# Joint weighted values for the narrow layers, a column bias from one product, a new table of context work, and transposed probabilities copied by ScalarE

## What is computed

```python
# narrow (layers 0 and 3)
q = (rmsnorm(x, norm_w) @ wq).reshape(B, T, 4, 4, 8)
scores = einsum('btgrd,bsgd->bgrts', q, k) / sqrt(8)
out = einsum('bgrts,bsgd->btgrd', softmax(scores), v).reshape(B, T, 128)
x = x + out @ wo
# wide (layers 1 and 2)
col_bias[:, token_indices_A] = -20 * (1 - mask_A)   # one value a row
col_bias[:, token_indices_B] = -20 * (1 - mask_B)   # B wins over A
probs = softmax(q @ k^T / 8 + col_bias)
x = x + (probs @ v) @ Wo + bo
```

## Time and profile before

| | us |
|---|---|
| median of 3 runs | 409.97 (409.69 to 411.9) |
| profiled execution | 409.9 |
| its span, first to last instruction | 408.1 |
| TensorE busy in the span | 380.6 (93%) |
| VectorE, ScalarE, GpSimd busy | 278.2 (68%), 265.8 (65%), 206.7 (51%) |

### The profile page before, as it was taken

The page is one execution under the profiler, slowest core; times in us unless marked ns, Lnnn a source line. Parts: engine busy times, 40 slices in busy tenths (PEclk is TensorE's granted clock), DMA queues, the critical chain, the costliest instruction groups (busy, mean ns, idle before and its releaser), DMA issues.

```text
span 408.1 us, 10552 instructions
## 1 busy us (share of the span) xinstructions
PE 380.6 (93%) x3552; PEld 331.2 (81%) x3552; DVE 278.2 (68%) x1430; ACT 265.8 (65%) x1143; POOL 206.7 (51%) x238
## 2 busy tenths in 40 slices
PE   7999596999999999989999999999999999987775
PEld 6877495899899988968868878888999898866564
DVE  3769955456555756578668877668757756688983
ACT  4585657586657657557477777688777656655870
POOL 5766643254323334468476676345333334567841
PEclk9599898999999999999999999999999999999989
DMA  8700150000000000000000000000000000000000
GB/s 257 323 2 2 45 214 1 2 2 2 2 0 2 2 2 2 2 2 0 2 9 7 8 9 3 0 2 2 2 2 2 2 2 2 0 2 3 6 8 13
DMA packets 4739, 9.71 MB, mean 24 GB/s; under 512 B 592, under 2 KB 3152, under 8 KB 4432
## 3 DMA queue, kind: packets, MB, share of 16 engines
q1 hardware_dynamic: 4400, 8.72, 5.9%
q10 hardware_dynamic: 288, 0.33, 0.3%
HBM read 8.53 MB, written 0.52 MB: 22 GB/s over the span
## 4 chain that ended last, share of the span: by engine, by line
PE 81%; DVE 11%; issue 3%; ACT 3%; DMA 1%; SPq 0%; DVEq 0%
PE pt_ps L791 13%; PE scores_ps L778 9%; PE v_ps L840 8%; PE fill_ps L656 8%; PE fill_ps L658 8%; PE fill_ps L657 8%; PE q_ps L745 7%; PE v_ps L810 7%; PE v_ps L822 7%; PE scores_ps L765 6%; DVE probs L577 6%; ACT probs L462 2%; DVE probsT L588 2%; DVE oT L595 1%; DMA smalls<-in_small 1%
## 5 line engine op out<-in xcount | busy, mean ns | idle before, releaser
L462 ACT ACTIVATE probs<-probs,negmax 128x128 f32<-128x128 f32 x512 | 198.4, 389 | 114.3 <-DVE negmax L577 114.3
L356 POOL TENSOR_TENSOR probs<-probs,inv 128x512 f32<-128x512 f32 x128 | 134.8, 1054 | 186.0 <-DVE inv L584 185.1
L462 ACT ACTIVATION_READ_ACCUMULATOR probs<-probs,negmax 128x1 f32 x512 | 95.6, 187 | 0.0
L577 DVE CUSTOM_DVE_ANT_0 probs<-scores_ps,col_bias,inv_rms 128x128 f32<-128x128 f32 x256 | 73.5, 346 | 21.3 <-PE scores_ps L765 21.1
L577 DVE CUSTOM_DVE_ANT_0 probs<-scores_ps,col_bias 128x128 f32<-128x128 f32 x256 | 58.2, 284 | 41.9 <-PE scores_ps L778 41.9
L588 DVE COPY probsT<-pt_ps 128x512 f32<-128x512 f32 x128 | 82.3, 684 | 5.4 <-PE pt_ps L791 3.4
L791 PE MATMUL pt_ps<-smalls,probs 128*128 128x128 f32 x512 | 72.2, 286 | 0.0
L791 PEld LDWEIGHTS pt_ps<-smalls,probs 128*128 128x128 f32 x512 | 57.0, 145 | 12.6 <-issue 11.3
L810 PE MATMUL v_ps<-probsT,v_narrow 128*32 128x128 f32 x512 | 36.2, 286 | 11.9 <-issue 8.2
L810 PEld LDWEIGHTS v_ps<-probsT,v_narrow 128*32 128x32 f32 x512 | 27.2, 113 | 21.8 <-issue 16.4
L577 DVE DVE_READ_ACCUMULATOR2_ANT negmax<- 128x1 f32 x512 | 43.4, 85 | 0.0
(11 more groups left out here) (90 smaller groups left out, 582.5 us busy)
## 6 DMA issues: line engine op xcount, KB each, us to landing
kT<-in_kv_w SPq DMA_DIRECT2D x6, 512.0 KB, 6.9
w_qo<-in_qo_w SPq DMA_DIRECT2D x2, 1024.0 KB, 9.8
v<-in_ctxT SPq DMA_DIRECT2D x4, 256.0 KB, 3.8
v<-in_kv_w SPq DMA_DIRECT2D x2, 512.0 KB, 11.1
outT<-x SPq DMA_DIRECT2D x8, 64.0 KB, 1.6
x<-in_xT SPq DMA_DIRECT2D x1, 384.0 KB, 8.2
oT<-in_narrow_kv ACTq DMA_DIRECT2D x1, 320.0 KB, 3.0
wn<-in_narrow_w SPq DMA_DIRECT2D x2, 128.0 KB, 4.9
```

Source lines behind the costliest of these rows:

```text
L356: nc.gpsimd.tensor_tensor(p4, p4, inv[:, o % 2, side, :].unsqueeze(2).broadcast_to([P, 4, S]), ALU.mult,).then_inc(probs_made[side], 1)
L462: last = nc.scalar.activation(e, e, ACT.Exp, scale=-1.0, bias=negmax[:, o % 2, side, q:q + 1], accum_out=rowsum[:, o % 2, side, q:q + 1])
L577: last = nc.vector.tensor_tensor_reduce(out=probs[:, o % PROBS_RING, side, cols], in0=scores_ps[side][:, cols], in1=bias, scale=scale, sca ...
```

## The change

It does six things.

- Narrow weighted values are issued once per job, for both octets: 16 products in turn over four column groups, in the half of octet o = 2n + 4. probsT gets a second buffer, by the parity of the octet, for this.
- ScalarE copies the second side of the transposes of all narrow octets, between its first and second four exponentials; VectorE keeps the first side, and both sides of wide octets.
- The column bias: each partition compares its own index (a new column of the small constants) with the tokens, four diagonals are made from it, and one product with mean_w (all 1/128) on TensorE, an entry "bias" in FILLS, spreads them over all rows. VectorE scales the result by 128 x 20 x (1 - mask). bias_made comes after octet 5, SyncE's wait for it is gone, and so are the iota and the comparison of all keys.
- FILLS has other octets for most entries, and the splits of pieces 6 and 7 come an octet later on VectorE, that of piece 0 after octet 0's scores.
- Context 1 is rounded by ScalarE ahead of the loop.
- kn_raw is gone: raw narrow keys go to kn_lo, which is split in place; ScalarE waits for kd_made of the keys two before in place of kn_split. The narrow bias is a broadcast zero (no_bias).

```diff
@@ -78,16 +78,16 @@
...
-    0: ["vn0", "k0.0"], 1: ["kn1.0", "k0.1", "k0.2"], 2: ["k0.3", "v0.0"], 3: ["v0.1", "v0.2", "vn1"],
...
-    24: ["k4.0"], 25: ["k4.1", "kn2.0"], 26: ["k4.2", "vn3"], 27: ["k4.3", "v4.0"], 28: ["v4.1"], 29: ["v4.2", "kn3.0", "v4.3"],
-    30: ["k5.0"], 31: ["k5.1", "k5.2"], 32: ["k5.3"], 33: ["v5.0", "v5.1"], 34: ["v5.2"], 35: ["v5.3", "k6.0"],
...
+    0: ["vn0"], 1: ["k0.0", "kn1.0"], 2: ["k0.1", "k0.2"], 3: ["k0.3", "v0.0"], 4: ["vn1", "v0.1"],
+    5: ["v0.2", "bias"], 6: ["v0.3", "k1.0"], 7: ["k1.1", "k1.2"],
+    8: ["k1.3"], 9: ["v1.0"], 10: ["v1.1", "kn0.3"], 11: ["v1.2", "vn2"], 12: ["v1.3", "k2.0"], 13: ["k2.1"],
...
+    24: ["v3.3"], 25: ["k4.0", "kn2.0"], 26: ["k4.1", "vn3"], 27: ["k4.2"], 28: ["k4.3"], 29: ["v4.0", "kn3.0"],
+    30: ["v4.1", "v4.2"], 31: ["v4.3"], 32: ["k5.0", "k5.1"], 33: ["k5.2"], 34: ["k5.3", "v5.0"], 35: ["v5.1"],
...
+    41: ["v6.1"], 43: ["kn2.3", "v6.2"], 44: ["v6.3"], 45: ["k7.0"], 46: ["k7.1"], 47: ["k7.2"], 48: ["k7.3"],
+    50: ["v7.0"], 53: ["v7.1", "kn3.3"], 55: ["v7.2"], 57: ["v7.3"],
...
@@ -190,7 +191,7 @@
         probs = sb("probs", [P, PROBS_RING, 2, BANK])
-        probsT = sb("probsT", [P, 2, BANK])
+        probsT = sb("probsT", [P, 2, 2, BANK])
         negmax = sb("negmax", [P, 2, 2, 4])
@@ -243,6 +242,10 @@
             return 0 <= o < 2 * NJOBS
+
+        def scalar_copy(o):
+
+            return valid(o) and is_narrow(o // 2)
@@ -268,7 +271,6 @@
             piece(5)
-            sp.wait_ge(bias_made, 1)
             context(2)
@@ -286,8 +288,9 @@
-                pool.wait_ge(c_loaded[p], 16)
-                nc.gpsimd.tensor_copy(c_hi[:, p], c_in[p]).then_inc(rest_rounded, 1)
+                if p > 1:
+                    pool.wait_ge(c_loaded[p], 16)
+                    nc.gpsimd.tensor_copy(c_hi[:, p], c_in[p]).then_inc(rest_rounded, 1)
                 pool.wait_ge(rest_rounded, p)
@@ -313,9 +318,9 @@
                 pool.wait_ge(fill_read[fill_bank(name)], fill_count(name))
-                nc.gpsimd.tensor_copy(kn_hi[:, i % 2], kn_raw[:]).then_inc(kn_rounded, 1)
+                nc.gpsimd.tensor_copy(kn_hi[:, i % 2], kn_lo[:, i % 2]).then_inc(kn_rounded, 1)
                 pool.wait_ge(kn_rounded, i + 1)
-                nc.gpsimd.tensor_tensor(kn_lo[:, i % 2], kn_raw[:], kn_hi[:, i % 2].bitcast(F32), ALU.subtract
+                nc.gpsimd.tensor_tensor(kn_lo[:, i % 2], kn_lo[:, i % 2], kn_hi[:, i % 2].bitcast(F32), ALU.subtract
                                         ).then_inc(kn_split, 1)
@@ -425,9 +429,11 @@
                         return
-                    if i > 1:
-                        act.wait_ge(kn_split, i)
-                    nc.scalar.activation(kn_raw[:], source[:, 0:PAIR], ACT.Copy).then_inc(fill_read[bank], 1)
+                    if i >= 2:
+                        before = KN_ORDER[i - 2]
+                        last = max(n for n, (l, b) in enumerate(JOBS) if f"kn{b // 2}.{l}" == before)
+                        act.wait_ge(kd_made, 2 * narrow_index(last) + 2)
+                    nc.scalar.activation(kn_lo[:, i % 2], source[:, 0:PAIR], ACT.Copy).then_inc(fill_read[bank], 1)
                     return
@@ -470,9 +476,14 @@
                 for name in FILLS.get(o - 1, [])[1:]:
-                    fill_out(name)
+                    if name != "bias":
+                        fill_out(name)
                 if valid(o):
                     exponentials(o, 0)
+                if scalar_copy(o - 2):
+                    act.wait_ge(pt_full[1], o - 1)
+                    nc.scalar.activation(probsT[:, o % 2, 1, :], pt_ps[1][:], ACT.Copy).then_inc(pt_read[1], 1)
+                if valid(o):
                     exponentials(o, 1)
@@ -491,6 +502,8 @@
             round_piece(1)
+            act.wait_ge(c_loaded[1], 16)
+            nc.scalar.activation(c_hi[:, 1], c_in[1], ACT.Copy).then_inc(rest_rounded, 1)
             for n, h in HALVES:
@@ -512,27 +525,29 @@
-                dve.wait_ge(keys_made, 1)
                 dve.wait_ge(tokens_loaded, 16)
-                setup(nc.vector.tensor_copy(key_f, key_i[:]))
                 setup(nc.vector.tensor_copy(tok_f[:, :, 0:2], tok_i[:]))
...
                 setup(nc.vector.tensor_scalar(tok_f[:, :, 2:4], tok_f[:, :, 0:2], float(S), None, ALU.add))
-                shape = [P, LAYER_MASKS, S, 4]
-                setup(nc.vector.tensor_tensor(equal, key_f.unsqueeze(1).unsqueeze(3).broadcast_to(shape),
-                                              tok_f[:].unsqueeze(2).broadcast_to(shape), ALU.is_equal))
+                setup(nc.vector.tensor_scalar(tok_f[:], tok_f[:], key_index, None, ALU.is_equal))
+                setup(nc.vector.tensor_reduce(hits[:].rearrange("p l m -> p (l m)"), tok_f[:], mybir.AxisListType.X, ALU.max))
+                setup(nc.vector.tensor_scalar(only_a[:], hits[:, :, 1], -1.0, 1.0, ALU.mult, ALU.add))
+                setup(nc.vector.tensor_tensor(only_a[:], only_a[:], hits[:, :, 0], ALU.mult))
+                for j in range(4):
+                    on = hits[:, j, 1:2] if j < 2 else only_a[:, j - 2:j - 1]
+                    nc.vector.tensor_scalar(diagonals[:, j, :], identity, on, None, ALU.mult).then_inc(diagonals_made, 1)
...
-                setup(nc.vector.tensor_reduce(hits, equal, mybir.AxisListType.X, ALU.max))
-                of_mask = hits.rearrange("p (l m) s -> p m l s", m=2)
-                setup(nc.vector.tensor_scalar(suppress[:], mask, -SUPPRESS, SUPPRESS, ALU.mult, ALU.add))
-                setup(nc.vector.tensor_scalar(free, of_mask[:, 1], -1.0, 1.0, ALU.mult, ALU.add))
-                setup(nc.vector.tensor_tensor(free, free, of_mask[:, 0], ALU.mult))
-                setup(nc.vector.tensor_scalar(col_bias[:, 0:2, :], of_mask[:, 1], suppress[:, 1:2], None, ALU.mult))
+                bank = fill_bank("bias")
+                setup(nc.vector.tensor_scalar(suppress[:], mask, -SUPPRESS * C, SUPPRESS * C, ALU.mult, ALU.add))
+                dve.wait_ge(fill_full[bank], fill_count("bias"))
+                columns = fill_ps[bank][:].rearrange("p (j s) -> p j s", j=4)
+                setup(nc.vector.tensor_scalar(col_bias[:], columns[:, 0:2], suppress[:, 1:2], None, ALU.mult))
                 setup(nc.vector.scalar_tensor_tensor(
-                    out=col_bias[:, 0:2, :], in0=free, scalar=suppress[:, 0:1], in1=col_bias[:, 0:2, :],
+                    out=col_bias[:], in0=columns[:, 2:4], scalar=suppress[:, 0:1], in1=col_bias[:],
                     op0=ALU.mult, op1=ALU.add))
+                dve.sem_inc(fill_read[bank], 1)
                 dve.sem_inc(bias_made, 1)
@@ -567,7 +582,7 @@
                 l, b = job(n)
-                bias = col_bias[:, 2 if l in NARROW else l - 1, :]
+                bias = no_bias[:].broadcast_to([P, S]) if l in NARROW else col_bias[:, l - 1, :]
                 scale = inv_rms[:, n % 2:n % 2 + 1] if l in NARROW else 1.0
@@ -585,7 +600,7 @@
                 dve.wait_ge(pt_full[side], o + 1)
-                nc.vector.tensor_copy(probsT[:, side, :], pt_ps[side][:]).then_inc(pt_read[side], 1)
+                nc.vector.tensor_copy(probsT[:, o % 2, side, :], pt_ps[side][:]).then_inc(pt_read[side], 1)
@@ -622,19 +637,22 @@
                     transposes_out(o - 2, 0)
-                    transposes_out(o - 2, 1)
+                    if not scalar_copy(o - 2):
+                        transposes_out(o - 2, 1)
+                if o == 0:
+                    split_piece(0)
                 if valid(o):
...
                     match_tokens()
-                if o == 4:
+                if o == 5:
                     column_bias()
-                if o in (5, 6):
-                    split_piece(o + 1)
-
-            nc.vector.memset(col_bias[:, 2, :], 0.0)
+                if o in (6, 7):
+                    split_piece(o)
+
+            nc.vector.memset(no_bias[:], 0.0)
             dve.wait_ge(smalls_loaded, 16)
@@ -688,6 +705,9 @@
                                                 start=(c == 0), stop=(c == CC - 1))
+                elif name == "bias":
+                    pe.wait_ge(diagonals_made, 4)
+                    last = nc.tensor.matmul(out[:], mean_w[:], diagonals.rearrange("p j s -> p (j s)"), start=True, stop=True)
                 elif name.startswith("kn"):
@@ -794,9 +814,11 @@
                 l, b = job(n)
-                if n > 0 and (h == 0 or l not in NARROW):
+                if l in NARROW and h == 0:
+                    return
+                if n > 0:
                     pe.wait_ge(v_read, uses(n, h) - 1)
-                if h == 0 and n > 0:
+                if n > 0 and (h == 0 or l in NARROW):
                     pe.wait_ge(y_read, n)
@@ -804,14 +826,13 @@
                     for r in range(REP):
-                        for side in range(2):
-                            rows = slice(32 * (2 * h + side), 32 * (2 * h + side) + 32)
+                        for g in range(KV_HEADS):
```

(19 more changed lines are left out.)

22 lines of the change are left out of this document (9 added, 13 removed), and 10 rows, old and new, of the table FILLS.

## The result

The changed kernel takes **388.73 us** (median of 4 runs, 383.08 to 390.74) against 410.08 of the kernel before on the same chip (4 runs, 409.69 to 411.9). The ratio is 0.939, 95% interval 0.931 to 0.947: faster by 5 to 7%. It leaves out the two executions of 390.69 and 390.74 us as slow ones, over 1.5% above the fastest; by medians it would be 0.948. The forecast was 383 with a range of 375 to 394; it holds the result, 5.7 us above its middle.

A forecast was written before the change was run, and what follows sets the result against it. TensorE's own work bounds the middle, waits the two ends; 8.9 before the first scores + front 46 + middle 270 + end 56 = 380.9 us of span, 382.7 with 1.8 around it, said as 383; range 376 to 388, with rivals 375 to 394.

The forecast's parts named there:

- Joint values, 1.00 a job instead of 2.00: Narrow weighted values on TensorE: a job's 32 records over four column groups side by side take 1.00 us, not 2.00.
- Middle, 270.0: Octets 8 to 53: 275.3 us before, -9.0 values, +2.8 fills, +3.4 floor, -2.5 idling at the wide-to-narrow turn.
- The floor that I costed at +3.4: Odd narrow octets 27, 31, 33, 35, 37: VectorE's rows and queries take 4.0 us, TensorE 3.3; 5 x 0.7.
- ScalarE's copies at no cost in the middle: Second-side copies moved from VectorE to ScalarE in narrow octets: cost 0 in the middle, with 0.7 us of cover.
- Front, 46: Octets 0 to 7: 63.9 us before, -10.5 stalls, -5.6 fills, -3.0 values, +0.9 bias product; 45.7, taken as 46.
- The stalls' 10.5: Front: TensorE's waits of 4.21 and 3.10 us for the residual add, plus 1.68 and 1.55 at low clock, go.
- End, 56.0: From octet 54, 60.0 us before: +0.2 in octets 54 to 58, -1.7 in 59 to 62, -2.5 behind the last scores.
- 1 (the front keeps its waits): Front: ScalarE is full, copies queue and fills wait for banks; half the 10.5 stays, 388 to 390 us; chance 0.13.
- 2: Narrow values: four column groups don't overlap, values cost 2.0 us a job; +11, 394 us; chance 0.08.
- 3: Slower: ScalarE's copy lands late and holds up narrow octets' values and transposes; 412 us; chance 0.02.
- 4: No gain: joint products still pair (+11) and the odd octets' floor is 5 us, not 4 (+16); 410 us; chance 0.02.
- 5: Better: no floor in the odd octets and the front at ScalarE's pace; 376 us; chance 0.04.

The follow-up runs named there:

- the swap: Changed kernel without products, wide fills in octet pairs 30/31 to 36/37 put one in the even octet and two in the odd; 382.6 us.
- the set-up alone: Changed kernel with the old context table, values per octet and both copies on VectorE, leaving new column bias, no SyncE wait, context 1 on ScalarE, later splits; 406.85 us.
- the kernel with products: Changed kernel plus eight TensorE products of 128 columns that nothing reads behind each of octets 59, 61 and 63; 382.9 us.

## Why the prediction came out as it did

**Joint values, 1.00 a job instead of 2.00: right.** Measured 1.02. The way to it was half right: I took two groups' gain as a law for four; the runs give 0.46 of the 1.00 to the four groups. The Trainium skill, "TensorE: Matmul & The Clock Gate", section on measured speedup against the span model, has 3.07 times for four row tiles, from which 1.17 is an estimate. The trace does not agree for this shape: 32 records over four column groups take 1.02.

**Middle, 270.0: right, 270.4**, by the terms. Pairs 6.4 and 4.1 us, five floors of 0.67 (forecast 0.7), TensorE idle 3.5 in all (270.43 less 266.92). The floor that I costed at +3.4 was real and avoidable: the swap took 3.0 of it back.

**ScalarE's copies at no cost in the middle: right as a cost, wrong as a worth.** They save 3.9 there, since the joint values would otherwise wait for VectorE's second copy. The sum held because it assumed no wait before the values in either case.

**Front, 46: right, 45.8 and 43.8.** The stalls' 10.5 is confirmed in place and nearly in size (8.8 by the set-up alone). ScalarE was busy 39.2 us there, not the 42.1 forecast. Of six profiles of this same front, five have 43.3 to 43.8, so 46 was 2 too long for most. What the sum did not say is how much rests on the table: the three parts alone add up to the whole, but all parts without the table are worth only 1.5. The bank waits on ScalarE above are what the trace shows for it; which of the other parts makes them longer is not separated.

**End, 56.0: wrong in the profiled execution, 62.2.** This is the step that failed. The chain was right: octets 59 to 62 at 4.06 to 4.09 us with the clock up (forecast 3.9 to 4.0), and 56.9 in all. The term "where a longer fall of the clock would cost 1 to 2" was mis-sized: it costs 5.2 (62.1 less 56.9), and seven of the changed kernel's ten executions have a mean clock of 0.978 or less, where the kernel with products has 0.988 or more. I had the row for it, clock 0.96 in the last stretch of the earlier trace rows, and the arithmetic: taking 1.00 of values out of octets that already idled 1.08 doubles the idling. I booked the shorter chain and not what less work does to the clock. The same row hid a second error: the 17.4 us that four octets took before were not VectorE's chain alone, since octet 62 ran at 0.70 and took 5.01. At the full clock the same four take 16.6 with both copies on VectorE and 16.3 with one on ScalarE, so ScalarE's copies are worth 0.3 there and not 1.7.

**The range.** 388.73 lies 0.7 outside the inner range, 376 to 388. The outer one, 375 to 394, holds it by the room made for rivals 1 and 2, and neither of them happened: that part of the hit is luck.

**Rivals.** 1 (the front keeps its waits) forecast 388 to 390, which is the measured time for another reason: its stalls are gone. 2 is out by the values' 1.02. 3 and 4 are out: TensorE never waits on ScalarE's copy in the middle. It does once in the front (0.20 us) and twice behind octet 63 (2.59 and 0.89, the first 0.82 when the clock is up), where it waited for VectorE's copies before, so this one of the signs of being wrong showed without the harm. 5 is out too: the floor is there.

## What to carry to other kernels

When an edit takes work off the engine whose clock follows its work, count the idle time it leaves stage by stage, and price the low clock over what follows; here four products that nothing reads, 0.9 us in each of three octets, were worth five. When parts of a change are timed one by one, compare them stage by stage, and take each out of the whole as well as adding it to the old: table, set-up and joint values were worth 1.4 to 4.6 us of time alone and 21 to 23 together with ScalarE's copies, though on the front they simply added up; the table was worth 6.1 us of the front alone, and 19.1 as the last part added (62.4 less the 43.3 of its base). And where one half of a loop has a floor set by another engine, give the free work to that half.

## What the runs showed of the hardware

- The clock fell in seven of eight octets that followed one with 2.05 to 2.08 us of TensorE idling, in four of eight that followed 1.01 to 1.09, and in none with products in the gap, of which one kernel left 1.19 (mean clock 0.991 in six executions of six). At the 1.2 GHz level eight transposes took 1.97 for 1.09, 32 records of values 1.94 for 1.08.
- The time of the changed kernel went from 382.8 us at a mean granted clock of 0.986 to 390.3 at 0.963; with eight products it went from 382.2 to 383.6, at 0.988 to 0.991. The kernel before also varies, from 405.3 to 413.0 in 29 executions, at 0.991 to 0.968.
- Products of two pairs of column groups, issued one pair after the other, overlap by themselves: 1.54 us for the two, not 2.0; the second pair's first record starts 0.47 us after the first pair's. Issued in rotation, 32 records over four groups take 1.02 to 1.08.
